# Attention on one TensorE: the four maxima products of a key tile issued one by one between values and scores, and six buffers for the exponentials

## The reference, cut to what is touched

```python
scores = jnp.einsum('bqhd,bkhd->bhqk', q, k) * scale
probs = jax.nn.softmax(scores, axis=-1)
out = jnp.einsum('bhqk,bkhd->bqhd', probs, v).reshape(B, T, d)
```

## Time and profile before

| | us |
|---|---|
| median of three runs | 3699.14 (3696.56 to 3699.18) |
| span of the profiled execution | 3662.3 |
| median less that span | 36.8 |
| main stretch of the attention, clock at full rate | 303.4 to 1559.8 |
| last key tiles, no first pass left | 1559.8 to 1608 |

### The profile page before, as it was taken

One profiled execution on the slowest core, in us unless ns is written; L12 is line 12 of the kernel. 1 busy time (PEld: TensorE's weight loads), 2 busy tenths in 40 slices (PEclk: granted clock), 3 DMA queues, 4 the chain that ended last, 5 costly groups with the idle time before them and its releaser, 6 DMA issues. The chain is left out here.

```text
span 3662.3 us, 87949 instructions
## 1 busy us (share of the span) xinstructions
PE 3233.5 (88%) x34874; PEld 1861.3 (51%) x34875; DVE 2951.6 (81%) x4783; ACT 2058.3 (56%) x2972; POOL 1196.7 (33%) x974
## 2 busy tenths in 40 slices
PE   4899999999999999984999766996899999967776
PEld 1543333333333333344666542432777887756665
DVE  5778999999999999926666354775799999958986
ACT  0317777777777777762111264665675756434553
POOL 0310000000000000006011560000899999927875
PEclk8869999999999999996999877998999999989998
DMA  1561112020202030027222363333543434231110
GB/s 58 189 174 9 29 22 45 5 45 5 46 10 59 19 56 6 5 70 277 62 65 65 91 207 106 135 119 133 147 128 111 142 108 133 68 126 47 57 35 18
DMA packets 223121, 296.00 MB, mean 81 GB/s; under 512 B 72872, under 2 KB 159536, under 8 KB 220592
## 3 DMA queue, kind: packets, MB, share of 16 engines
q1 hardware_dynamic: 211616, 264.14, 25.5%
q0 software_dynamic: 6144, 17.05, 1.4%
q10 hardware_dynamic: 5008, 9.80, 0.7%
HBM read 174.35 MB, written 115.95 MB: 79 GB/s over the span
## 5 line engine op out<-in xcount | busy, mean ns | idle before, releaser
L1015 DVE TENSOR_REDUCE att_maxima<-att_ps_m 128x1 f32<-128x512 f32 x2048 | 1286.0, 685 | 58.0 <-PE att_ps_m L1071 55.3
L970 ACT ACTIVATE att_probs<-att_ps_s 128x1024 f32<-128x1024 f32 x1024 | 999.4, 1021 | 284.1 <-PE att_ps_o L1100 271.2
L1100 PE MATMUL att_ps_o<-att_probs,held_vs 128*32 128x256 f32 x8192 | 659.2, 394 | 4.7 <-ACT att_probs L970 0.6
L2456 POOL TENSOR_TENSOR ss_ch<-ss_h,ss_c_rep 128x1024 f32<-128x1024 f32 x256 | 601.7, 2441 | 10.1 <-DVE ss_h L2543 10.1
L1071 PE MATMUL att_ps_m<-held_ks,held_qs 48*128 48x512 f32 x2048 | 585.0, 512 | 5.4 <-PEq L60 4.6
L2575 PE MATMUL ss_ps_u<-ss_diag,ss_dx_t 128*32 128x128 f32 x16384 | 475.8, 274 | 32.3 <-DMA ss_dx_t<-scratch_dx_t 16.1
L2575 PEld LDWEIGHTS ss_ps_u<-ss_diag,ss_dx_t 128*32 128x32 f32 x16384 | 455.3, 110 | 86.4 <-issue 71.1
L1071 PEld LDWEIGHTS att_ps_m<-held_ks,held_qs 48*128 48x128 f32 x2048 | 238.6, 188 | 449.6 <-DVE att_maxima L1015 391.5
L1086 PE MATMUL att_ps_s<-held_qs,held_ks 50*128 50x512 f32 x2048 | 454.8, 405 | 2.8 <-ACT att_probs L970 1.0
L2495 ACT ACTIVATE ss_decay<-ss_delta,ss_a_neg 128x1024 f32<-128x1024 f32 x256 | 293.8, 1148 | 229.4 <-DVE ss_h L2543 213.2
L1100 PEld LDWEIGHTS att_ps_o<-att_probs,held_vs 128*32 128x32 f32 x8192 | 162.8, 108 | 362.2 <-issue 340.9
(11 more groups left out here) (394 smaller groups left out, 4483.6 us busy)
## 6 DMA issues: line engine op xcount, KB each, us to landing
ss_delta<-scratch_delta SPq DMA_DIRECT2D x256, 128.0 KB, 3.1
held_qs<-scratch_q SPq DMA_DIRECT2D x96, 128.0 KB, 4.7
held_ks<-scratch_k SPq DMA_DIRECT2D x96, 128.0 KB, 5.1
ex_x<-scratch_sorted_x SPq DMA_DIRECT2D x72, 132.0 KB, 2.1
scratch_sorted_y<-ex_y SPq DMA_DIRECT2D x72, 128.0 KB, 1.7
scratch_q<-held_parts SPq DMA_DIRECT2D x16, 512.0 KB, 4.6
scratch_k<-held_parts SPq DMA_DIRECT2D x16, 512.0 KB, 5.2
moe_w_w<-in_W SPq DMA_DIRECT2D x16, 512.0 KB
```

The source lines that it names most:

```text
L970: act.activation(probs[:, (2 * n + pair) % 4, :, :], ps_s[pair][:, :, :], ACT.Exp, scale=HD ** -0.5).then_inc(exp_done, 1)
L1015: dve.tensor_reduce(maxima[:, j, at:at + 1], ps_m[plan.bank(key)][:, :], AX.X, ALU.max).then_inc(maxed, 1)
L1100: mm = pe.matmul(ps_o[h * VW:(h + 1) * VW, cols], vs[st // QC % 2][:, kt, h * VW:(h + 1) * VW], probs[:, (2 * n + h // 2) % 4, h % 2, cols ...
L2456: pool.tensor_tensor(ch[:, w.n % (CH_GROUPS * DQ), :], h[:, w.n % H_SLOTS, :], c_rep[:, w.ng, :], ALU.mult).then_inc(s["ch_ready"], 1)
```

## The change

The four blocks of the first pass no longer stand in pairs ahead of the scores. In each half tile one stands before the two score products and one behind them. `probs` has six slots, so that the exponentials of tile n wait for the values of tile n-3.

```diff
+PROBS = 6
...
-        probs = r.sb("probs", [P, 4, 2, GN])
+        probs = r.sb("probs", [P, PROBS, 2, GN])
...
-                    if n >= 2:
-                        act.wait_ge(pv_done, n - 1)
+                    if n >= PROBS // 2:
+                        act.wait_ge(pv_done, n - PROBS // 2 + 1)
                     act.wait_ge(shifted, 2 * n + pair + 1)
-                    act.activation(probs[:, (2 * n + pair) % 4, :, :], ps_s[pair][:, :, :], ACT.Exp, scale=HD ** -0.5).then_inc(exp_done, 1)
+                    act.activation(probs[:, (2 * n + pair) % PROBS, :, :], ps_s[pair][:, :, :], ACT.Exp, scale=HD ** -0.5).then_inc(exp_done, 1)
...
-                                       probs[:, (2 * n + h // 2) % 4, h % 2, cols], start=(kt, half) == (0, 0), stop=(kt, half) == (KT - 1, 1))
+                                       probs[:, (2 * n + h // 2) % PROBS, h % 2, cols], start=(kt, half) == (0, 0), stop=(kt, half) == (KT - 1, 1))
...
                         last_values(st, kt, 0)
                         if s < STEPS:
                             first_pass(s, i, 0)
+                        next_scores(st, kt, 0)
+                        if s < STEPS:
                             first_pass(s, i, 1)
-                        next_scores(st, kt, 0)
                         last_values(st, kt, 1)
                         if s < STEPS:
                             first_pass(s, i, 2)
+                        next_scores(st, kt, 1)
+                        if s < STEPS:
                             first_pass(s, i, 3)
-                        next_scores(st, kt, 1)
```

## The result

| | before | after |
|---|---|---|
| median, ten runs each, same chip (us) | 3696.18 | 3673.51 |
| ratio, with its 95% interval | | 0.9948 (0.9936 to 0.9961) |
| profiled execution: span (us) | 3662.3 | 3668.8 |
| a step, between two `shift_of` (us) | 41.90 | 41.41 |
| last `shift_of` to last reciprocal (us) | 48.6 | 44.7 |

The kernel became faster by 22.7 us, 0.5% (14 to 24 by the interval). The forecast was 48. The direction and the main idea held; more than half of the gain is missing. (The profiled execution of after has the longer span although the kernel is faster: pieces outside the attention, which the change doesn't touch, took longer. The output projection behind it, from its first to its last instruction, took 131.6 us, where two later executions of the same kernel take 100.5 and 100.2. So from here on the attention is compared stretch by stretch, and medians with medians.)

What follows compares the result with a forecast made beforehand. A loop through TensorE and VectorE, not either engine alone, was taken as the bound. Profiled span 3662.3 less 44.5 for the steps and tiles ahead, less 4 behind the last block, plus 36.8 outside: 3651 us; range 3635 to 3780.

Steps and rivals of the forecast that it cites:

- the turn of the maxima: Where `shift_of` holds VectorE 0.22 us against 0.18 of room: 0.1 us a step left for late blocks, besides 0.20 itself.
- the pairing: Upper-row and lower-row products on TensorE still run beside each other in the new order: two slots a half tile, not three.
- Rival 1: Pairing lost on TensorE: each half tile gets a lone slot of 0.23 us, 3875 us in all; chance 0.16.
- Rival 2: Lower scores start only after the upper block's load, about 0.11 us later: half tile 1.34, about 3755 us; chance 0.10.
- Rival 4: VectorE becomes the bound at once, its reads meeting TensorE's writes; only the tail is won: 3695 us; chance 0.04.
- The loop through the bank: Block, its maximum, then the block three places on: bank free at 1.28 us, holding two old half tiles to about 2.51.
- TensorE's own 1.23 is what is late next: With the loop open by 0.18 us, TensorE sets each half tile at 1.23 us; VectorE needs 1.20.
- Nothing is added: The new order keeps the same products, loads and VectorE work, and passes no DMA or queue of SyncE or GpSimd.
- ScalarE gets its scores without that wait: A block waiting for its bank now has the values behind it, so it no longer delays the scores for ScalarE.
- The tail: Behind the first pass's last block, six slots cut a tile from 2.2 to 2.0 us: 4 us over 20 tiles.
- With the 36.8 around it: Time outside the profiled span, 36.8 us, added to the forecast span of 3614 us to give 3651 us.
- Rival 3: TensorE really needs 1.25 us a half tile; only two late blocks a step and the tail are won: 3675 us; chance 0.12.

Runs made afterwards that it cites:

- the third order: Kernel after with both blocks of a half tile as a pair behind the two score products: 3672.09 us against 3663.46 of the kernel before, ratio 1.0024.
- The mended version: Kernel after with key tile 1's first block pair ahead of the scores and the maxima's turn one group of values later: 3635.52 us, ratio 0.9924 to the kernel before.

## Why the prediction was right or wrong, point by point

**What failed, in one place.** Of the 43.5 us forecast for the steps 13.8 came. Three terms of the sum were wrong, by size: the turn of the maxima (0.1 left for it, 0.49 measured, 12 us), the half tile (1.23, measured 1.24, 10 us), and a wait of the scores for an exponential that the sum did not have at all (0, measured 0.24, 7 us). The last is a mistake of mechanism, the first in part, the second of size alone.

**The sign, and the pairing: right.** The argument went from the values' passes, which overtake each other on column strips, to the halves of the rows. It held, and the half tile of two slots is in the trace. Rival 1 gave the right price for a third slot (0.23, measured 0.22 to 0.23), but its case did not come. Here trace and page part: the order of starts that the Trainium skill states in "TensorE: Matmul & The Clock Gate", Part 3, "What overlaps and what doesn't", is not what these rows show, and the measurement decides. Rival 2 (1.34) did not come either: the lower score starts 0.00 to 0.01 behind the upper block. Its condition is real all the same: where the wait is not yet met, the load holds back what stands behind it (770.50, 808.78). The argument from the values' passes was weaker than it reads. The trace shows their starts, and not the order in which they stand in the program; and that they carry no wait is not so for the first load of a group, which has the one of L1094. For the halves of the rows the evidence is in the trace of after. Rival 4 is out as VectorE has room, 1.20 against 1.24.

**The loop through the bank: right.** It was worked out from starts, durations and one load; the third order brought it back on purpose, with half tiles of 1.23 and 1.28 and the late block. It was not taken away alone, with a fourth bank.

**"TensorE's own 1.23 is what is late next": off by 0.01.** It is 1.24. The 1.23 was read from the half tile right behind a hold-up; the bounds had allowed for that (0.015). The old half tile was 1.257 on the mean ((41.88 - 0.99 of turns and copy - 0.68 of two late blocks) / 32). So 0.01 x 32 = 0.32 a step or 10 us is missing here.

**"Nothing is added", and "ScalarE gets its scores without that wait": wrong in mechanism.** It is true of the instructions, not of the waits. The prediction asked of the block that was moved back what it waits for and who waits for it. It did not ask so of the scores, which were moved ahead by 0.33. Once a step they now stand before an exponential that ScalarE starts late, because of its copy of the outputs: 0.24 a step, 7 us. The row that names this copy was in hand and was used for the other wait at the same place, 0.20. None of the rivals has this mechanism. The mended version showed it: undone in one key tile out of 16, the step lost 0.24. The third order, which also has the scores right behind the values, shows the same wait.

**"I leave 0.1 for it", at the turn of the maxima: 0.49, the largest miss.** The estimate counted VectorE's 0.22 for `shift_of` against 0.18 of room. It left out that the turned maxima occupy one of the three banks. So the turn itself waits for a maximum (0.28 of the 0.49), and a block behind it needs the maximum of one block later than usual (0.17 with what follows). Before, the two late blocks of the earlier trace rows cost 0.68; the change won 0.19 of it, not 0.58. 0.39 a step, 12 us.

Together 0.32 + 0.24 + 0.39 + 0.01 for the copy = 0.96, which is 41.41 - 40.45. Over 30 steps that is 29 us of the 48.

**The tail: right**, 4 us, and by itself (48.6 to 44.7 with the slots alone).

**"With the 36.8 around it": wrong, though it changed nothing in the difference.** An execution takes 1.8 us more than its span (3670.53 against 3668.8). The 36.8 were the distance between a profiled execution and others: the kernel before has medians of 3696.18 and 3663.46 on two chips, and single times that differ by 19 us on one (3653.65 to 3673.04). Two profiled executions of the kernel after on two chips differ by 25.8 us in span (3668.8 and 3643.0) and by 0.1 in the attention (1375.6 and 1375.5): that difference lies inside the span, in stretches that the change does not touch. For the kernel before on its first chip no execution of 3696 was profiled, so there the same is likely and not shown.

**Rival 3 came nearest in size** (3675 against 3673.51, with 24 us of gain), by luck and for another reason than it gave: it let the half tile stay at 1.25 and both late blocks vanish. In truth the half tile fell to 1.24, a new wait came, and most of the old one at the turn stayed.

## What to carry to other kernels

When two instructions change places, ask both of them what they wait for, also the one that comes earlier: a wait that was just covered becomes visible, and here its row was the one already used for its neighbour. A pace read right behind a hold-up was too short here; take it from a stretch of many, less the places that are counted apart, and price a shared buffer by its users, the odd one among them too. Where two engines are both near 100%, work out the loop through the buffers from starts; it told here which order has the faster half tile. It did not tell how the third order compares with the first: that was decided by two waits at the start of a step.

## What the runs showed of the hardware that was not expected

- **The clock stayed down.** With three of four row-bound products on one half of the rows, TensorE was granted 1.2 GHz (0.50) from 207 to 2914 us while it was listed as busy all the time (1000.00 of 1000 us from 1000 to 2000). The same change in one unit of 16 left it at 1.00. Each is one execution. What sets the clock is not settled: the run only shows that a TensorE listed as busy is not enough, and that a difference in how the rows are used can go with some 1100 us.
- **The moment of its rise is not fixed.** 274 to 322 us in executions of nearly the same program, and an extra product behind each pair in the opening did not bring it forward (282 us with it and without).
- **Products on different halves of the rows overtake each other** (lower scores at 766.32, upper ones at 766.66), as long as the wait of the one passed is already met. Where it is not, the load holds back the loads behind it, also those of the other half (770.50 in after, 808.78 in before). On one half they keep their order, at 0.22 to 0.23 us for each that finds no partner.
